# Row loads over 48 partitions, and the last sequence's attention tail moved into the experts' first turn

## The reference

```python
a = jnp.einsum('bqhd,bkhd->bhqk', q, k) / Dh ** 0.5        # 16 heads of 8
a = jnp.where(mask, a, NEG_INF)                             # causal
a = jax.nn.softmax(a, axis=-1)
o = jnp.einsum('bhqk,bkhd->bqhd', a, v)
return jnp.einsum('blhe,hed->bld', o, Wout)
...
probs = jax.nn.softmax(t @ gate_w.T, axis=-1)
topw, topi = jax.lax.top_k(probs, K)                        # 2 of 8 experts
h1 = base1[None] + SCALING * jnp.einsum('etr,efr->etf', jnp.einsum('td,erd->etr', t, a1), b1)
act = jax.nn.silu(h1) * h3
out_e = jnp.einsum('etf,df->etd', act, w2) + SCALING * jnp.einsum('etr,edr->etd', jnp.einsum('etf,erf->etr', act, a2), b2)
```

## Time and profile before

| | |
|---|---|
| median of 3 runs | 1116.33 us (1116.32 to 1117.96) |
| profiled execution, its own time | 1120.27 us |
| span of its instructions | 1118.5 us |
| busy TensorE, VectorE, ScalarE, GpSimd | 921.9, 781.9, 517.0, 465.7 us |
| mean granted TensorE clock | 0.922 of 2.4 GHz |
| DMA in the attention stage | 0.30 to 0.36 of 16 engines, 84 to 107 GB/s |
| row loads | 32 of qS, 32 of kS, 204 KB each |

### The profile page before, as it was taken

One profiled execution on the slowest core, in us unless ns is written; L12 is line 12 of the kernel. 1 busy time (PEld: TensorE's weight loads), 2 busy tenths in 40 slices (PEclk: granted clock), 3 DMA queues, 4 the chain that ended last, 5 costly groups with the idle time before them and its releaser, 6 DMA issues. The chain is left out here.

```text
span 1118.5 us, 18158 instructions
## 1 busy us (share of the span) xinstructions
PE 921.9 (82%) x6169; PEld 549.5 (49%) x6169; DVE 781.9 (70%) x1507; ACT 517.0 (46%) x755; POOL 465.7 (42%) x629
## 2 busy tenths in 40 slices
PE   6899999994476666457999888978839999999997
PEld 2445555552354444333444443434326776677765
DVE  6777777775688999367778786868545666666642
ACT  3666666785123334324767665756713122232221
POOL 3112222224345556612555564535434335453344
PEclk9999999998668889767999999989968999999999
DMA  9000000000000000343333332310000000000000
GB/s 287 18 10 10 9 9 9 9 0 20 9 20 9 9 26 10 86 123 104 98 91 90 95 101 82 94 71 5 12 1 11 20 7 12 19 19 19 9 1 19
DMA packets 36254, 46.25 MB, mean 41 GB/s; under 512 B 4134, under 2 KB 27174, under 8 KB 36190
## 3 DMA queue, kind: packets, MB, share of 16 engines
q1 hardware_dynamic: 36189, 45.41, 13.5%
HBM read 22.00 MB, written 15.27 MB: 33 GB/s over the span
## 5 line engine op out<-in xcount | busy, mean ns | idle before, releaser
L1553 ACT ACTIVATE PT<-PS 128x1024 f32<-128x1024 f32 x160 | 162.9, 1022 | 87.1 <-PE PS L1333 87.1
L1609 POOL TENSOR_SCALAR_AFFINE_SELECT PT<-PT 128x256 f32<-128x256 f32 (+1 forms) x224 | 95.0, 439 | 147.6 <-ACT PT L1553 146.5
L1948 POOL TENSOR_TENSOR PRE_sb<-PRE_sb,VA 128x512 f32<-128x512 f32 x64 | 82.2, 1284 | 146.8 <-DVE PRE_sb L1996 146.7
L1922 ACT ACTIVATE sg_d<-PS 128x512 f32<-128x512 f32 x64 | 38.2, 597 | 183.8 <-PE PS L1070 183.7
L1647 DVE TENSOR_REDUCE negm<-PS 128x2 f32<-128x1024 f32 x64 | 78.0, 1225 | 44.1 <-PE PS L1322 42.6
L356 ACT ACTIVATE E<-PS,m 128x512 f32<-128x512 f32 x128 | 86.2, 684 | 40.3 <-PE PS L281 25.5
L1996 DVE TENSOR_TENSOR PRE_sb<-sg_d,PS 128x512 f32<-128x512 f32 x64 | 43.5, 687 | 82.6 <-ACT sg_d L1922 81.3
L1348 PE MATMUL PS<-PT,VA 128*32 128x512 f32 (+3 forms) x1024 | 92.7, 459 | 3.3 <-POOL PT L1609 3.3
L1318 PE MATMUL PS<-kS,qS 51*128 51x384 bf16 (+3 forms) x512 | 75.9, 319 | 22.0 <-DVE spread L1750 8.6
L469 DVE TENSOR_SCALAR E<-E 128x512 f32<-128x512 f32 x128 | 68.6, 536 | 33.5 <-ACT E L356 29.7
L387 POOL TENSOR_SCALAR Qs<-Qs 128x1024 f32<-128x1024 f32 x32 | 35.0, 1096 | 116.2 <-ACT Qs L344 116.2
(11 more groups left out here) (269 smaller groups left out, 2130.1 us busy)
## 6 DMA issues: line engine op xcount, KB each, us to landing
qS<-qk_rows SPq DMA_DIRECT2D x32, 204.0 KB
kS<-qk_rows SPq DMA_DIRECT2D x32, 204.0 KB
qk_rows<-parts SPq DMA_DIRECT2D x32, 192.0 KB, 2.8
xs_sb<-XN_sb SPq DMA_DIRECT2D x23, 256.0 KB, 2.3
qk_rows<-parts SPq DMA_DIRECT2D x32, 128.0 KB, 2.8
X_sb<-in_x_dram SPq DMA_DIRECT2D x8, 256.0 KB, 6.8
gs<-PRE_sb SPq DMA_DIRECT2D x8, 256.0 KB, 2.3
qk_rows<-parts SPq DMA_DIRECT2D x32, 64.0 KB, 2.5
```

The source lines that it names most:

```text
L1553: nc.scalar.activation(PT[:, quad % 2, u, :], PS[:, b:b + 2, :].rearrange("p b n -> p (b n)"), ACT.Exp).then_inc(exp_ready, 1)
L1609: nc.gpsimd.affine_select(out=v, in_=v, pattern=[[0, 4 if u == 4 else 2], [1, P]], compare_op=ALU.is_ge, fill=0.0, base=0, channel_multipl ...
L1948: nc.gpsimd.tensor_tensor(acts[:, s, f, :], acts[:, s, f, :], W[:, slot, s, :], ALU.mult).then_inc(weighted, 1)
```

## The change

1. `qk_rows` has 48 rows. The loads move 48 partitions; the maxima products use 48 rows and need no zeros; the score products still use 51. The ones are written into kS once (four copies in place of eight).
2. The masked operands of sequence 0 are made by VectorE in the last period of `attention1`, behind the mask copies.
3. The tail of the last sequence (turns, divide, project, add, statistics, factor, apply) stands in the first turn of `ffn1`, in PSUM bank 1 instead of bank 0. The copy of the last quad is ScalarE's third instruction of the block, ahead of the activation table's load.
4. The low halves of w3 and b3 are made by VectorE instead of GpSimd.

The last four pieces of the diff are of `ffn1`: TensorE, ScalarE, GpSimd, VectorE.

```diff
-        self.qk_rows = nc.dram_tensor("qk_rows", [2, 2, 2, 51, NPAIR * S], BF16, kind="Internal").ap()
+        self.qk_rows = nc.dram_tensor("qk_rows", [2, 2, 2, 6 * DH, NPAIR * S], BF16, kind="Internal").ap()
...
-            own, heads = slice(64 * par, 64 * par + 51), slice(4 * h, 4 * h + 4)
+            own, heads = slice(64 * par, 64 * par + 6 * DH), slice(4 * h, 4 * h + 4)
...
             for slot in range(2):
-                for m in range(2):
-                    for par in range(2):
-                        sp.dma_start(pr.qk_rows[slot, m, par, 48:51, :].rearrange("r (a s) -> r a s", a=NPAIR),
-                                     pr.fixed[:, m, :].unsqueeze(1).broadcast_to([3, NPAIR, S])).then_inc(fixed_out, 16)
+                for par in range(2):
+                    sp.dma_start(pr.kS[64 * par + 48:64 * par + 51, slot, :, :],
+                                 pr.ones[:, :].unsqueeze(1).broadcast_to([3, NPAIR, S])).then_inc(fixed_out, 16)
...
                     for j, col, k in both:
-                        q, key = operands(slot, quad, j)
+                        q, key = operands(slot, quad, j, 48)
...
             weighted_v(LAST, LAST % 2, 3, (3, 2))
-            pe.wait_ge(m_kept, 4)
-            turn_ot(LAST, 3)
-            turn_on(LAST)
-            project_out(LAST)
...
+            def mask_first_high(k):
+                dve.wait_ge(ex.first_u_kept, 3)
+                dve.wait_ge(m_kept, k + 1)
+                dve.wait_ge(s_ready, LAST * 20)
+                for m in range(2):
+                    ins = nc.vector.tensor_tensor(ex.umh[:, 0, m, k, :], ex.uh[:, m, :], ex.M[:, 0, k, :], ALU.mult)
+                ins.then_inc(ex.umh_ready, 1)
...
+                    elif last and (quad, u) in ((2, 1), (3, 0)):
+                        mask_first_high(quad - 2)
+                    elif last and (quad, u) in ((2, 4), (3, 1)):
+                        mask_first_low(quad - 2)
...
+                    if first and n == 5:
+                        pe.wait_ge(att_added, NB)
                     hidden(i, slot, n)
+                    if first and n == 0:
+                        turn_ot()
+                    elif first and n == 2:
+                        project_out()
                     if n == 0 and not last:
                         turn_x(i + 1)
-                    elif n == 1:
+                    if first and n == 1:
+                        turn_on()
+                    if n == 1:
...
-            nc.scalar.preload_act_table_set("silu_and_others")
             for whole, (high, low) in split:
                 nc.scalar.activation(high[:], whole[:], ACT.Copy).then_inc(const_high, 1)
+            act.wait_ge(ex.pv_ready, NB * 4)
+            nc.scalar.activation(OTs[:, :], PS[:, 7, :], ACT.Copy).then_inc(ot_kept, 1)
+            nc.scalar.preload_act_table_set("silu_and_others")
...
+                    if is_seq(i, 0) and n == 4:
+                        factor()
...
+                    if first and n == 0:
+                        divide()
+                    elif first and n == 2:
+                        add_att()
+                    elif first and n == 6:
+                        apply()
```

More of the change, by code:

```diff
@@ L1285, in _, with operands @@
         def _(pe):
-            def operands(slot, quad, j):
-                own = slice(64 * (j % 2), 64 * (j % 2) + 51)
+            def operands(slot, quad, j, rows):
+                own = slice(64 * (j % 2), 64 * (j % 2) + rows)
                 return qS[own, slot, 2 * quad + j // 2, :], kS[own, slot, 2 * quad + j // 2, :]
@@ L1638, in _ @@
             in_periods(pool, period)
-            factor(LAST)
         @block.vector
@@ L1755, in _ @@
             in_periods(dve, period)
-            divide(LAST, 3)
-            add(LAST)
-            apply(LAST)
 def ffn1(nc, g, out):
@@ L1875, in down, with to_bank1, turn_ot, turn_on @@
                 ins.then_inc(out_ready, 1)
+            def to_bank1(src, done):
+                for t in range(NT):
+                    ins = nc.tensor.transpose(PS[:, 1, t * P:(t + 1) * P], src(t), g.ident[:])
+                ins.then_inc(done, 1)
+            def turn_ot():
+                pe.wait_ge(ot_kept, NB * 4)
+                to_bank1(lambda t: OTs[:, t * P:(t + 1) * P], ot_turned)
+            def turn_on():
+                pe.wait_ge(o_normed, NB * 4)
+                to_bank1(lambda t: on[:, t, :, :].rearrange("p h e -> p (h e)"), on_turned)
+            def project_out():
+                pe.wait_ge(onT_ready, NB)
+                for t in range(NT):
+                    ins = nc.tensor.matmul(PS[:, 1, t * P:(t + 1) * P], onT[:, t * P:(t + 1) * P], g.wout1[:, :], start=True, stop=True)
+                ins.then_inc(att_ready, 1)
             def turn(i, slot):
@@ L1914, in keep_mask, with keep_on @@
                 nc.scalar.activation(ex.mask_kept(slot, k), PS[:, MASK_BANKS[k], :], ACT.Copy).then_inc(m_kept, 1)
+            def keep_on():
+                act.wait_ge(on_turned, NB)
+                nc.scalar.activation(onT[:, :], PS[:, 1, :], ACT.Copy).then_inc(onT_ready, 1)
             def turn(i, slot):
@@ L1922, in turn @@
                     nc.scalar.activation(sg[:, n % 2, :], PS[:, 4 + 2 * (f % 2), :], ACT.Silu).then_inc(silu_ready, 1)
+                    if first and n == 1:
+                        keep_on()
                     if last:
@@ L1951, in turn @@
                         nc.gpsimd.tensor_tensor(asum[:, f, :], acts[:, 0, f, :], acts[:, 1, f, :], ALU.add).then_inc(asum_ready, 1)
-            for n, (whole, (high, low)) in enumerate(split):
-                pool.wait_ge(const_high, n + 1)
-                nc.gpsimd.tensor_tensor(low[:], whole[:], high[:].bitcast(F32), ALU.subtract).then_inc(const_low, 1)
             in_pairs(pool, turn)
@@ L2013, in turn @@
                 mask_c(i, slot)
-            for k in range(2):
-                for m in range(2):
-                    nc.vector.tensor_tensor(umh[:, 0, m, k, :], uh[:, m, :], M[:, 0, k, :], ALU.mult).then_inc(first_masked, 1)
-                dve.wait_ge(first_masked, 4 * k + 2)
-                dve.sem_inc(umh_ready, 1)
-                for m in range(2):
-                    nc.vector.tensor_tensor(uml[:, 0, m, k, :], ul[:, m, :], M[:, 0, k, :], ALU.mult).then_inc(first_masked, 1)
-                dve.wait_ge(first_masked, 4 * k + 4)
-                dve.sem_inc(uml_ready, 1)
+            for n, (whole, (high, low)) in enumerate(split):
+                dve.wait_ge(const_high, n + 1)
+                nc.vector.tensor_tensor(low[:], whole[:], high[:].bitcast(F32), ALU.subtract).then_inc(const_low, 1)
             in_pairs(dve, turn)
```

68 lines of the change are left out of this document (49 added, 19 removed).

## The result

The changed kernel takes 1073.15 us (median of 4 runs, 1071.98 to 1073.54) against 1116.32 us: ratio 0.9593, 95% interval [0.9562, 0.9625]. That is 43.2 us less. A second set of five runs on another chip gave 0.9601 [0.9577, 0.9624]. The prediction was 1073, its range 1063 to 1086.

What follows compares the result with a forecast made beforehand. Bound: TensorE, busy over four fifths of the span, and its waits, such as for late maxima copies. 7.2 + 19.0 + 19.5 (20.3 less 0.8) - 2.5 = 43.2 us; 1116.3 - 43.2 = 1073.1 us, range 1063 to 1086.

Steps and rivals of the forecast that it cites:

- (a): Prologue and attention periods: 48-partition row loads spread over more engines, saving 7.2 us of xs wait and 19.0 of stalls.
- reserve of 1.5 us: Attention periods: stalls summed to 20.5 us, 19.0 taken, as some idle would return as waits for VectorE's maxima.
- (b): Last attention period: masks made there on VectorE cost 0.8 us, mostly hidden by GpSimd's factor; 2.6 without that cover.
- (c): From attention's end to the first SiLU: 5.0 us left instead of 25.3, so 20.3 saved.
- (d): Experts' first turn: taking in the tail costs 2.5 us, range 0 to 4.5, with GpSimd ending last.
- apply 1.1: Experts' first turn: the apply on VectorE was priced at 1.1 us.
- about 1 us more to the first down product: Sign for (d): first SiLU to the turn's first down product about 1 us more than 23.9.
- forecast wait for the last sum: Sign for (d): a wait of 1 to 3 us for GpSimd's last sum, between first SiLU and first down product.
- VectorE in the stalls' place: Rival, attention periods: half of the 19 us returns as waits for VectorE's maxima; 1083 us, chance 0.11.
- Exclusion and factor adding up: Rival: last period's masks and factor add up (+2.8), first turn pays 4.5 (+2), clock falls (+2); 1080 us, chance 0.09.
- Loads not spread: Rival, row loads: the DMA share stays near 0.2 and (a) is worth nothing; 1099 us, chance 0.06.
- loads on fewer engines: Rival, row loads: 48-row loads run on fewer than three engines, maxima copies land later; about 1149 us, chance 0.03.

Runs made afterwards that it cites:

- e1: The kernel before with the rows part alone (48-row loads, ones written once), tail and masks where they were: 1087.71 us, ratio 0.9726.
- e5: The changed kernel with the eight masking multiplies back at the start of the experts' block: 1076.61 us, ratio 0.9611 to the kernel before.
- e7: The changed kernel with the second expert's four masking multiplies moved behind the third quad's division in the last period: 1069.85 us.
- e10: e8 with the factor and apply of the sequence before the last moved from the last period to the experts' block: 1068.48 us.
- e6: The changed kernel with the last sequence's factor and apply moved behind the work of the experts' first turn: 1071.12 us.
- e4: The changed kernel with each row load cut into one of 46 partitions and one of 2: 1165.15 us, ratio 1.0408 to the kernel before.
- e8: The changed kernel with the edits of e6 and e7 together, run twice: 1068.98 and 1069.07 us.

## Why the prediction was right, and where it wasn't

**(a) Prologue and stalls: right, a little small.** Forecast 7.2 and 19.0; the rows alone (e1) gave 7.5 and 20.9. Of the reserve of 1.5 us for stalls that come back as waits for the maxima little was needed: these waits are 10.4 us before and 10.9 after. What no term held is that the first turn of the experts was slower too, by 1.7 us, at a mean clock of 0.92 in before and 1.00 in e1, without a change of that turn's work. How much of it the rows bring each time isn't settled: of the kernel before there is one profile, and the clock falls differently between executions.

**(b) Masks in the last period: right, but for the clock.** 0.8 forecast, with GpSimd's factor as the cover. Its selects start 0.75 us later (after against e5), and e7 and e10 confirm the cover: with the copy early the selects hold TensorE 2.54 us, with the factor gone 0.29 and 0.19. What the term left out is half clock at the end of the period, which brings the difference of the two profiles to 1.8 us. The prediction's remark on the old masks calls GpSimd's two instructions beside them multiplies; they are the two subtractions of w3 and b3 (L1955), and the eight multiplies took 7.75 us beside them.

**(c) The path to the first SiLU: right.** 5.0 us left were forecast, 4.04 measured, since the twelve products ran at full clock. 21.3 us gone instead of 20.3. Of these e5 assigns 5.6 to the masks; the tail's own steps are most of the rest. Part 4 of the change, the low halves on VectorE, stands in all of these runs but e1 and was not measured alone.

**(d) The first turn: the net was near by a balance, and a step behind it was wrong.** Forecast 2.5, measured 2.1 against before. But against the same turn with rows alone (e1, 32.07 us) it pays 3.84 us, and the 1.7 of the clock covered the difference. Its parts: 1.1 for work that stays with everything late (e6, 33.20), 1.8 for the factor ahead of the sums, 0.9 for the apply. The failed line is "apply 1.1": it took 4.99, each of its four instructions 1.2 to 1.4 us, about as long as the GpSimd instruction beside it (1.24, a third of 3.73). I had looked for exclusion only in the masks. The Trainium skill, "SBUF — State Buffer" (part on who interferes with whom), names also tensor_scalar, the apply's operation, among those of VectorE that can take the ports GpSimd uses, the later one waiting for the whole instruction. The trace agrees: 4.99 us beside GpSimd, 1.11 in e6 where GpSimd is idle. The sign "about 1 us more to the first down product" seems to fail and holds: it was 23.25 us (790.13 to 813.38), 0.6 less than in before, but in e1, the same turn at clock 1.00, it is 22.13, so 1.1 us less. The forecast wait for the last sum, 1 to 3 us, is there with 1.52, though behind the first down product and not ahead of it.

**The rivals.** VectorE in the stalls' place: no, 10.4 and 10.9 us of such waits. Exclusion and factor adding up: in part. GpSimd's factor was 0.8 us longer beside the masks, not 2.8. But the first turn paid 3.84 us against e1, of the 4.5 that the rival gave it, and the clock fell behind the new wait of 2.89 us, for about 1 us where the rival had 2. The apply's exclusion was at a place that the rival didn't name. Other terms, (a) above all, made up for these. Loads not spread, and loads on fewer engines: not here, but e4 shows the second is real at 46 partitions: 1165 us where the rival had 1149. Its price per copy was near (13.4 us where 16 were worked out); that 12 copies would be waited for, for 56.2 us, was more than the 7 counted as surely late.

**The sum.** 43.2 us was forecast and 43.2 measured, which is closer than the terms, and this closeness is luck. In the profiles (a) by e1 was 2.2, (c) 1.0 and (d) 0.4 us better than forecast. Against that stand about 1 us of clock in the last period and 1.6 of the last turn, neither of them in the sum; without the stretch ahead of M the profiles are 44.2 us apart. The kernel before also scatters: its median was 1116.3, 1120.4, 1118.0 and 1120.6 us in four sets, and in the second set of the changed kernel the medians are 44.3 us apart.

## What to carry to other kernels

Read the DMA share of a load-only stretch: a low one with much data moving means few engines, and the partition count of the load decides it, so keep constant rows out of a load whose count then divides well. Here a small copy paid for the large ones ahead of it, and TensorE's idle was often, not always, paid again in clock. Two profiles differ by a us or two for that reason alone, so compare stretches that ran at the same clock. When work is moved under other work, price each instruction with its neighbour on the other engine: four tensor_scalar operations of VectorE took over four times as long beside GpSimd's multiplies, while VectorE's own two-input multiplies beside GpSimd's small operations lost little and made those slower.

## What the runs showed of the hardware that was not expected

- 46 partitions cost 92 us more than 45 in the same kernel (1165.15 and 1073.14 us): share 0.13 and 0.87.
- Four 128x128 tensor_scalar operations of VectorE took 4.99 us beside GpSimd's multiplies and 1.11 alone; a 128x1024 multiply with one operand in PSUM took 1.2 us beside those multiplies and beside GpSimd's 4-element operations alike.
- The other way round, GpSimd's 4-element operations went from 0.20 to 0.51 us and from 1.01 to 1.33 beside VectorE's two-operand multiplies on SBUF, which themselves took 0.68 instead of 0.65.
- After the same wait of 2.54 us in two executions of one kernel (e8) TensorE's granted clock was 1.00 in one and 0.50 in the other: 1.50 and 2.79 us for the same 24 products. After the same idle of 2.10 us it fell in one kernel and not in another, with 1.6 us between their last turns.
